# Weight preparation moved into the first round of layer 0, score and maximum banks lent in the first and last round of layer 1, its loop over two rounds, a re-ordered round

## The chip, the cores and the metric

One core of a Trainium2 chip runs the whole program. The metric is the device time of one execution in microseconds (us); the time before is the median of three runs.

## The reference

Sixteen sequences of 512 tokens with 128 features go through two layers, each of which adds an attention part and a feed-forward part to its input.

```python
xn = _layernorm(x)                       # layer 0
x = x + _L0_attn_ref(xn, ...) + _L0_ffn_ref(xn, ...)
xn = _layernorm(x)                       # layer 1
x = x + _L1_attn_ref(xn, ...) + _L1_ffn_ref(xn, ...)
```

`_L0_attn_ref` is a gated linear recurrence with 16 heads of 64 (products with Wq, Wk, Wv, Wg, a scan with a decay per head, Wo) followed by a GELU block. `_L0_ffn_ref` is a gated product with ternary weights, two hidden 512x512 products (h1, h2) and w3. `_L1_attn_ref` is gated linear attention with 4 heads in chunks; `_L1_ffn_ref` is softmax attention with 16 heads of 8 over 512 keys, a layer norm, and one of four expert blocks for each token.

## The kernel before, in words

The program has four parts, one after the other. **Setting up layer 0** (L655 to L737): a block loads the constants; `prepare_weights` (L41 to L98) brings the 3.9 MB of weights to be split in five chunks through two buffers, multiplies them with a bias vector on TensorE (L70, one column each, 36 products), scales them on ScalarE (L80), and splits them on VectorE into a rounded high part (L96) and a rest, the low part (L98); a third block adds the biases (L731 to L734). Each block ends with all engines together. **Layer 0** (`layer0_sequences`, L161) runs rounds -1 to 17: in a round the stages P, M, T and X work on different sequences, in the order that `layer0_order` writes out by hand. P is layer norm (`stats`, seven small POOL steps, `xn`), two transposes and four `gate` products; M the products with the scan (`v`, `k`, `g`, `q`), `wo` and `h1`. In round -1 only P lives. **Layer 1's attention** (`attention`, L890) works likewise in rounds -4 to 16. **The experts** (`experts`, L1787) work on the sorted tokens at the end.

A full round of `attention` has 32 positions p (`attention_order`, L771). Each begins with a `score` and a `max` step. `max` (stage B, for the next sequence): TensorE multiplies with 24 rows into the two MAX banks (L1307), VectorE takes the row maximum of both (L1597), and the next `max` product waits until it has. `score` (stage C): TensorE multiplies with 25 rows into the two SCORE banks (L1325), ScalarE takes the exponential (L1444), and the next `score` product waits for it. After them each position has other steps, put there by hand: `pv` (L1335, probabilities times values), `aoT` (L1343, a transpose, then L1603 and L1605 on VectorE), `h2` (L1196 to L1198, eight steps of two thirds of a dozen products, with a ScalarE copy after each odd one), `U` (L1247) and its states on VectorE (L1559 to L1564), `A` (L1257) with a mask on VectorE (L1569), `xT` (L1214), `mT` (L1313, the transpose of the maxima, with ScalarE's copy L1440), `oT` (L1282), `gwo` (L1289), and so on. Single banks for these are taken in turn from the ring 6, 7: there are 31 uses in a round, so that `gwo` (p=31) and `gz` (p=0 of the next round) both have bank 6, and `gz` waits until VectorE has read `gwo` (L1591).

In round -1 stage B lives and stage C does not, in round 15 stage C lives and stage B does not. In the rounds -1, 13, 14 and 15, `warm` steps stand at the even positions: five products (L1185) whose result nobody reads.

SyncE issues all loads and stores in the same order: after `mqklo` (p=19) the 24 stores `qk_st`, then the loads `Bld` for the next sequence, then `g1_ld` (two loads of 1 MB for the next `h2`). POOL issues the indirect stores `scatter` at p=31.

`run` (L1028) has the rounds -4 to 1 and 12 to 16 written out, and a loop whose body is one round for 2 to 11:

```python
for r in range(-4, 2):
    rounds(0, r, live(r))
with eng.Fori(2, BATCH - 4) as b:
    rounds(b, 0, order)
for r in range(BATCH - 4, BATCH + 1):
    rounds(0, r, live(r))
```

Of the kernel before, what the change touches and what calls it, by code (L numbers as in the profile page):

```python
# [40 lines left out]
def prepare_weights(nc, name, raw_dram, split_hi, split_lo, chunks, bias_products=None, psum_bias=None, by_dim=(), base=0):  # L41

    widest = max(n for _, n, _ in chunks)
    with ExitStack() as ctx:
        raw = [ctx.enter_context(nc.sbuf_tensor(f"{name}_raw{i}", [P, widest * P], F32)) for i in range(2)]
        loaded = [ctx.enter_context(nc.semaphore(f"{name}_loaded{i}")) for i in range(2)]
        multiplied = ctx.enter_context(nc.semaphore(f"{name}_multiplied"))  # L50
        scaled = ctx.enter_context(nc.semaphore(f"{name}_scaled"))
        hi_done = ctx.enter_context(nc.semaphore(f"{name}_hi_done"))
        lo_done = ctx.enter_context(nc.semaphore(f"{name}_lo_done"))
        block = ctx.enter_context(nc.Block())

        @block.sync
        def _(sp):
            for i, (first, n, _) in enumerate(chunks):
                if i >= 2:
                    sp.wait_ge(lo_done, i - 1)  # L60
                sp.dma_start(raw[i % 2][:, 0:n * P], raw_dram[:, first * P:(first + n) * P]).then_inc(loaded[i % 2], 16)

        @block.tensor
        def _(pe):
            for i, (first, n, _) in enumerate(chunks):
                pe.wait_ge(loaded[i % 2], 16 * (i // 2 + 1))
                for blk, col, vec in bias_products or []:
                    if first <= blk < first + n:
                        w = raw[i % 2][:, (blk - first) * P:(blk - first + 1) * P]
                        nc.tensor.matmul(psum_bias[:, col:col + 1], w, vec, start=True, stop=True)  # L70
                pe.drain().then_inc(multiplied, 1)

        @block.scalar
        def _(act):
            for i, (first, n, scale) in enumerate(chunks):
                w = raw[i % 2][:, 0:n * P]
                act.wait_ge(loaded[i % 2], 16 * (i // 2 + 1))
                act.wait_ge(multiplied, i + 1)
                if scale is not None:
                    nc.scalar.activation(w, w, ACT.Copy, scale=scale).then_inc(scaled, 1)  # L80
                else:
                    act.drain().then_inc(scaled, 1)

        @block.vector
        def _(dve):
            for i, (first, n, _) in enumerate(chunks):
                w = raw[i % 2][:, 0:n * P]
                at = slice((first - base) * P, (first - base + n) * P)
                if first in by_dim:
                    w = w.rearrange("p (g j d) -> p g d j", j=4, d=8)  # L90
                    hi, lo = (s[:, at].rearrange("p (g d j) -> p g d j", d=8, j=4) for s in (split_hi, split_lo))
                else:
                    hi, lo = split_hi[:, at], split_lo[:, at]
                dve.wait_ge(loaded[i % 2], 16 * (i // 2 + 1))
                dve.wait_ge(scaled, i + 1)
                nc.vector.tensor_copy(hi, w).then_inc(hi_done, 1)  # L96
                dve.wait_ge(hi_done, i + 1)
                nc.vector.tensor_tensor(lo, w, hi.bitcast(F32), ALU.subtract).then_inc(lo_done, 1)  # L98


# [11 lines left out]
PREP_ROUNDS, PREP_PER_ROUND = 3, 4  # L112

# [47 lines left out]
def layer0_sequences(nc, psum, w_hi, w_lo, w_plain, col, bias, half_bias, decay, rows, ident, s1_half, s12_half, minus_half, eps,  # L161
                     d_x, d_x1, d_g1, d_sorted, prep_chunks, table_parts):
    with ExitStack() as ctx:
# [11 lines left out]

        def blk(w, i):
            return w[:, i * P:(i + 1) * P]

        OUTS = 4
        xin = sb("xin", [P, TILES, P])  # L180
# [35 lines left out]
        ga = sb("ga", [P, HID, SEQ])  # L216
        pad = sb("pad", [P, 1, PAY])
        prep_raw = sb("prep_raw", [P, HID * P])
        prep = sb("prep", [P, 2, HID * P], F32R)
# [12 lines left out]
        sems("P_filled", "M_filled", "T_filled", "wo_done")  # L232
        sems("gate_t", "h0_hi", "v", "t", "g1", "hT_hi", "ga", "xT_hi", "yT_hi")
# [41 lines left out]
        def _(sp):  # L275
            def rounds(base, add, now):
# [7 lines left out]
                for stage, kind, i in now:  # L284
                    if stage == "W":
# [4 lines left out]
                        if kind == "prep_ld":  # L290
                            sp.wait_ge(S["prep_lo"], n)
# [9 lines left out]
                    elif kind == "x_ld":  # L301
                        sp.wait_ge(S["xn"], upto(stage, 1, 0))
# [23 lines left out]
        def _(pe):  # L326
            def rounds(base, add, now):
# [5 lines left out]
                def take(u):  # L333
# [3 lines left out]
                    for back in range(3):  # L337
# [5 lines left out]
                        if same:  # L343
                            s, per, k = FREE[same[-1]]
                            pe.wait_ge(S[s], upto(stage_of[same[-1]], per, k, back))
                            return

                def product(out, w_blocks, x_hi, x_lo):
                    last = 3 * len(w_blocks) - 1
                    n = 0  # L350
# [420 lines left out]
def attention_order():  # L771
# [77 lines left out]
    for p in WARM_AT:  # L849
        put(p, "idle", "warm")  # L850
# [1364 lines left out]
```

## Time and profile before

| what | us |
|---|---|
| median of three runs (2694.82 to 2701.45) | 2697.13 |
| the profiled execution | 2709.48 |
| its span | 2707.7 |
| set-up and round -1 of layer 0 | 0 to 74 |
| layer 0 | 74 to 937 |
| set-up of layer 1, its rounds -4 to -2 | 937 to 1053 |
| round -1 of layer 1 | 1053 to 1143.5 |
| rounds 0 to 14 | 1143.5 to 2451 |
| round 15 | 2451 to 2509 |
| round 16 and the experts | 2509 to 2707 |

The span runs from the first instruction to the last; 1.8 us of the profiled execution lie around it. Rows of a timeline give start, duration, engine, line, operation, and in brackets the idle time of the engine before it with what ended it. PEclk is TensorE's granted clock, 1.00 for 2.4 GHz and 0.50 for 1.2 GHz.

### The profile page before, as it was taken

To read this page: it belongs to the slowest core of one execution; us is meant where nothing else is said; L and a number is where in the kernel's file an instruction comes from. 1 tells how busy PE (TensorE), PEld (TensorE's weight loads), DVE (VectorE), ACT (ScalarE), POOL (GpSimd) and SP (SyncE) were. 2 spreads that over 40 slices of the span, in tenths; PEclk is the share of its full clock that TensorE was granted. 3 is DMA by queue.
4 is the path that set the end of the run, shared out by engine and by line. 5 is a ranking of instruction groups with operands and counts; after the bars stand their busy time and mean duration, and the time that the engine had idled before them with its cause. 6 is when DMAs were issued, how large, how long until landed. Compare 5 with 4: busy or idle time off the path is not lost. (4 is left out here: it accounts for less than half of the span.)

```text
span 2707.7 us, 45139 instructions
## 1 busy us (share of the span) xinstructions
PE 2422.3 (89%) x14582; PEld 1672.5 (62%) x14582; DVE 1933.5 (71%) x3706; ACT 1338.1 (49%) x1926; POOL 594.3 (22%) x630
## 2 busy tenths in 40 slices
PE   3899999999999946899999999999999999999596
PEld 2788888888888734654555545554555555554395
DVE  3889888888888713667777777777777777772375
ACT  1444444444444312265666656665666666555242
POOL 0021112111221100102222221213221221212287
PEclk9999999999999968999999999999999999999798
DMA  4334432233223133323343334333333233211463
GB/s 153 125 115 127 127 100 76 76 119 104 80 76 111 43 135 98 101 75 96 118 130 93 86 101 136 99 88 104 117 116 103 82 107 106 65 51 32 140 228 104
DMA packets 195550, 280.31 MB, mean 104 GB/s; under 512 B 21672, under 2 KB 151161, under 8 KB 186880
## 3 DMA queue, kind: packets, MB, share of 16 engines
q1 hardware_dynamic: 189952, 266.47, 32.8%
q0 software_dynamic: 5504, 12.63, 1.3%
q8 instruction: 53, 0.87, 0.1%
q14 instruction: 41, 0.34, 0.0%
HBM read 148.65 MB, written 131.91 MB: 104 GB/s over the span
## 5 line engine op out<-in xcount | busy, mean ns | idle before, releaser
L1597 DVE TENSOR_REDUCE c_row_max<-b_psum 128x2 f32<-128x1024 f32 x512 | 624.3, 1219 | 286.2 <-PE b_psum L1307 264.7
L1444 ACT ACTIVATE c_prob<-b_psum 128x1024 f32<-128x1024 f32 x512 | 524.1, 1024 | 388.0 <-PE b_psum L1325 384.4
L1307 PE MATMUL b_psum<-c_bk,c_bq 24*128 24x512 f32 x1024 | 261.8, 507 | 55.1 <-DVE c_row_max L1597 38.5
L1325 PE MATMUL b_psum<-c_cq,c_ck 25*128 25x512 f32 x1024 | 261.3, 505 | 36.4 <-ACT c_prob L1444 31.5
L1335 PE MATMUL b_psum<-c_prob,c_v_aug 128*32 128x512 f32 x2048 | 283.5, 627 | 0.3
L1325 PEld LDWEIGHTS b_psum<-c_cq,c_ck 25*128 25x128 f32 x1024 | 96.3, 185 | 218.1 <-ACT c_prob L1444 109.7
L353 PE MATMUL a_psum<-a_yT_hi,a_w_hi 128*128 128x512 f32 x512 | 206.8, 404 | 8.3 <-issue 5.9
L353 PE MATMUL a_psum<-a_yT_hi,a_w_lo 128*128 128x512 f32 x512 | 203.7, 398 | 0.0
L353 PE MATMUL a_psum<-a_yT_lo,a_w_hi 128*128 128x512 f32 x512 | 203.6, 398 | 0.0
L1307 PEld LDWEIGHTS b_psum<-c_bk,c_bq 24*128 24x128 f32 x1024 | 97.0, 186 | 108.1 <-DVE c_row_max L1597 82.1
L459 ACT ACTIVATE a_g<-a_psum,a_cols 128x512 f32<-128x512 f32 x64 | 44.1, 689 | 238.5 <-PE a_psum L353 238.5
L517 DVE TENSOR_TENSOR_SCAN a_st_sb<-a_decay,a_kv_sb 128x512 f32<-128x512 f32 x128 | 157.2, 1228 | 4.4
L615 POOL TENSOR_TENSOR a_rs<-a_mv,a_eps 128x4 f32<-128x4 f32 x16 | 3.2, 201 | 664.2 <-DVE a_mv L540 664.2
L376 PEld LDWEIGHTS a_psum<-a_w_plain,a_outs 128*128 128x128 f32 x1024 | 134.3, 192 | 11.8
L1196 PE MATMUL b_psum<-c_g_hi,b_f_hi 128*128 128x512 f32 x256 | 119.4, 467 | 17.7 <-DMA b_f_lo<-f_split_scratch 11.6
L376 PE MATMUL a_psum<-a_w_plain,a_outs 128*128 128x128 f32 x1024 | 135.0, 275 | 0.0
L1749 POOL TENSOR_TENSOR c_o_ms<-c_o_ms,b_minus_half 128x16 f32<-128x16 f32 x16 | 46.6, 2910 | 385.0 <-DVE c_o_ms L1581 385.0
L514 DVE SCALAR_TENSOR_TENSOR a_kv_sb<-a_psum,a_bias,a_v_sb 128x512 f32<-128x512 f32 x128 | 95.5, 746 | 44.0 <-PE a_psum L353 23.2
L353 PEld LDWEIGHTS a_psum<-a_yT_hi,a_w_hi 128*128 128x128 f32 x512 | 97.1, 190 | 29.8 <-issue 8.7
L447 ACT ACTIVATE a_v_sb<-a_psum,a_bias 128x512 f32<-128x512 f32 x128 | 88.7, 693 | 47.2 <-PE a_psum L353 46.2
L353 PEld LDWEIGHTS a_psum<-a_yT_lo,a_w_hi 128*128 128x128 f32 x512 | 97.6, 191 | 23.2
L353 PEld LDWEIGHTS a_psum<-a_yT_hi,a_w_lo 128*128 128x128 f32 x512 | 97.6, 191 | 21.2
(298 smaller groups left out, 5419.9 us busy)
## 6 DMA issues: line engine op xcount, KB each, us to landing
sorted_scratch<-a_pad SPq DMA_DIRECT2D x16, 2184.5 KB, 13.9
g_scratch<-a_g_hi SPq DMA_DIRECT2D x16, 1024.0 KB, 4.0
g_scratch<-a_g_lo SPq DMA_DIRECT2D x16, 1024.0 KB, 7.1
c_g_hi<-g_scratch SPq DMA_DIRECT2D x16, 1024.0 KB, 6.1
c_g_lo<-g_scratch SPq DMA_DIRECT2D x16, 1024.0 KB, 8.1
stack_scratch<-c_qk_hi SPq DMA_DIRECT2D x256, 64.0 KB, 1.6
d_wt<-expert_scratch SPq DMA_DIRECT2D x19, 834.0 KB
c_bq<-stack_scratch SPq DMA_DIRECT2D x128, 96.0 KB
```

The source lines that it names most:

```text
L353: mm = nc.tensor.matmul(out, a, c, start=(n == 0), stop=(n == last))
L376: mm = nc.tensor.matmul(tok[:, cut(t)], outs[:, i % OUTS, cut(t)], blk(w_plain, A_WO + i), start=(i == 0 and t == 0), stop=(i == FB0 - 1), ...
L447: nc.scalar.activation(v_sb[:, i % 2, :], bank(f"v{i}"), ACT.Identity, bias=bias[:, 4 * i:4 * i + 1]).then_inc(S["v"], 1)
L514: nc.vector.scalar_tensor_tensor(out=kv_sb[:, :], in0=bank(f"k{i}"), scalar=bias[:, 4 * i + 1:4 * i + 2], in1=v_sb[:, i % 2, :], op0=ALU.a ...
L517: nc.vector.tensor_tensor_scan(st_sb[:, :], decay[:, i:i + 1].to_broadcast([P, SEQ]), kv_sb[:, :], 0.0, ALU.mult, ALU.add).then_inc(S["sca ...
L1196: nc.tensor.matmul(bank(f"h2{c}"), hi, g1_hi[:, k, :], start=(k == 0), stop=False)
L1307: mm = nc.tensor.matmul(psum[:, MAX + x, :], bq[r, j, cut(t)], bk[r, j, :], start=True, stop=True)
L1325: mm = nc.tensor.matmul(psum[:, SCORE + x, :], ck[r, j, cut(kb)], cq[r, j, :], start=True, stop=True)
L1335: mm = nc.tensor.matmul(psum[32 * g:32 * g + 32, PV, :], v_aug[:, kb, HPG * j + g, :], prob[:, (2 * i + g // 2) % 4, g % 2, :], start=(kb ...
L1444: nc.scalar.activation(prob[:, i % 4, :, :], psum[:, SCORE:SCORE + 2, :], ACT.Exp, scale=DH1 ** -0.5).then_inc(S["exp"], 1)
L1597: nc.vector.tensor_reduce(row_max[:, t, at:at + 3:2], psum[:, MAX:MAX + 2, :], AX.X, ALU.max).then_inc(S["row_max"], 1)
L1749: nc.gpsimd.tensor_tensor(o_ms[:, 2, :], o_ms[:, 1, :], minus_half[:, :], ALU.pow).then_inc(S["o_rms"], 1)
```

## The change

Four things are done at once.

1. `prepare_weights` and the three set-up blocks of layer 0 go. SyncE issues the columns, the first input tile, the identity and all weight chunks at once, each with a semaphore and a place of its own. The high parts (ScalarE), the low parts (VectorE) and the bias products (TensorE) stand behind steps of round -1; round 0 begins with the bias sums.
2. In round -1 of layer 1 the odd `max` steps use the SCORE banks, in round 15 the odd `score` steps use the MAX banks; the product then waits for the reader of two steps before. `warm` stands at every fourth position in round -1, at the even ones in 13 and 14, and nowhere in round 15.
3. The loop's body holds two rounds; it runs five times in place of ten.
4. In every round of layer 1: the `h2` steps at even p stand first among the steps of their position and after `pv`, `ao` and `aoT` of stage C (before `aoT` of stage C2 at p=4, before `aT` at 6, before `xT` at 16), the one of p=14 moves to the end of p=13; `mT` 0 moves from 17 to 22, its store from 19 to 24; the second `oT` from 29 to 30. The banks up to `O1` are turned round: `gz` has bank 7, `gwo` bank 6, and the two neighbours in one bank are now `O1` and `mT` 0.

```diff
+WEIGHTS = {"s": (A_S1, 2 * HID, None), "q1": (0, 2 * FB0, "ln1_g"), "q2": (2 * FB0, 2 * FB0, "ln1_g"), "h1": (A_H1, HID * HID, None),
+           "w1": (A_W1, HID, "ln2_g")}
+HIGH_BEHIND = {("stats", 0): ("s", "q1", "q2"), ("gate", 0): ("h1",), ("gate", 1): ("w1",)}
+LOW_BEHIND = {("stats", 0): ("s",), ("xn", 0): ("q1",), ("gate", 0): ("q2",), ("gate", 1): ("h1",), ("gate", 2): ("w1",)}
+BIAS_BEHIND = {("stats", 0): range(0, 8), ("xT", 0): range(8, 12), ("gate", 0): range(12, 18), ("gate", 1): range(18, 24),
+               ("gate", 2): range(24, 30), ("gate", 3): range(30, 36)}
...
+            sp.dma_start(cols[:, :], d_cols).then_inc(S["cols_in"], 16)
+            sp.dma_start(xin[:, :, :], x_rows[0]).then_inc(S["x_in"], 16)
+            sp.dma_start(ident[:, :], d_ident).then_inc(S["ident_in"], 16)
+            for name in WEIGHTS:
+                sp.dma_start(raw_of[name], weight(d_split, name)).then_inc(S["raw_" + name], 16)
+            sp.dma_start(w_plain[:, :], d_plain[:, 0:A_W3 * P]).then_inc(S["plain_in"], 16)
+            sp.dma_start(rows[:, :, :], d_rows).then_inc(S["rows_in"], 16)
...
+                        nc.scalar.activation(weight(w_hi, name), raw_of[name], ACT.Copy,
+                                             scale=col(by) if by else 1.0).then_inc(S["w_hi"], 1)
...
+                        nc.vector.scalar_tensor_tensor(out=weight(w_lo, name), in0=raw_of[name], scalar=col(by) if by else 1.0,
+                                                       in1=weight(w_hi, name).bitcast(F32), op0=ALU.mult,
+                                                       op1=ALU.subtract).then_inc(S["w_lo"], 1)
...
-H2_AT = (2, 4, 6, 10, 14, 16, 19, 20)
+H2_AT = (2, 4, 6, 10, 13, 16, 19, 20)
...
+    for n, p in enumerate(H2_AT):
+        if p % 2 == 0:
+            put(p, "F", "h2", n)
     put(0, "C2", "xnb_ld")
...
-    put(17, "B", "mT", 0)
+    put(22, "B", "mT", 0)
...
-    put(19, "B", "m_st", 0)
+    put(24, "B", "m_st", 0)
...
-    put(29, "A1", "oT", 1)
+    put(30, "A1", "oT", 1)
...
+        bank_of |= {u: RING[(n + 1) % 2] for n, u in enumerate(ring_uses[:ring_uses.index("O1") + 1])}
...
-            few = r == -1 or BATCH - 3 <= r < BATCH
-            return [step for step in order if (few if step[0] == "idle" else 0 <= r + OUT_OF[step[0]] < BATCH)]
+            every = {-1: 4, BATCH - 3: 2, BATCH - 2: 2}.get(r)
+            return [step for step in order
+                    if (every and step[2] % every == 0 if step[0] == "idle" else 0 <= r + OUT_OF[step[0]] < BATCH)]
...
-            with eng.Fori(2, BATCH - 4) as b:
+            with eng.Fori(2, BATCH - 5, 2) as b:
                 rounds(b, 0, order)
+                rounds(b, 1, order)
...
-                        pe.wait_ge(S["row_max"], upto(stage, PAIRS, i))
+                        alone = not looped and add == -1
+                        pe.wait_ge(S["row_max"], upto(stage, PAIRS, i - 1 if alone else i))
...
-                        pe.wait_ge(S["exp"], upto(stage, PAIRS, i))
+                        alone = not looped and add == BATCH - 1
+                        pe.wait_ge(S["exp"], upto(stage, PAIRS, i - 1 if alone and i else i))
```

## Rows read from the trace of the kernel before

**Rows 1.** The page: the span of the profiled execution.
```profile
span 2707.7 us, 45139 instructions
```
**Rows 2.** Busy time by stretch: length, busy time of each engine, PEclk, DMA share, GB/s.
```profile
0.00:74.10 74.10, 25.83 (x104) 21.77 (x104) 27.68 (x52) 13.55 (x16) 3.23 (x11) 1.00 0.47 146
...
1053.30:1143.50 90.20, 78.13 (x393) 53.65 (x393) 55.72 (x72) 24.18 (x39) 10.10 (x8) 0.92 0.33 95
...
2451.40:2509.00 57.60, 54.79 (x300) 25.44 (x298) 9.88 (x45) 34.59 (x37) 10.97 (x13) 1.00 0.10 31
```
**Rows 3.** Timeline of the start, all engines.
```profile
13.20 14.04 PE L70 MATMUL a_psum<-a_cols,a_raw 128*128 128x1 f32 x64 [13.20 <-DMA a_raw<-in_a_split]
...
27.36 2.00 ACT L80 ACTIVATE a_raw<-a_raw,a_cols 128x2048 f32<-128x2048 f32 x1 [5.05 <-PEq L71]
...
43.22 2.29 DVE L98 TENSOR_TENSOR a_w_lo<-a_raw,a_w_hi 128x2048 fp32r<-128x2048 f32 x1
...
47.58 0.50 SPq L303 DMA_DIRECT2D a_xin<-in_x  x1
...
51.55 0.87 DVE L535 BATCH_NORM_STATS2 a_stats<-a_xin 128x6 f32<-128x128 f32 x4 [4.44 <-DMA a_xin<-in_x]
...
61.28 0.76 PE L353 MATMUL a_psum<-a_xT_hi,a_w_hi 128*128 128x512 f32 x1 [1.49 <-DVE a_xT_lo L502]
...
74.19 0.47 PE L353 MATMUL a_psum<-a_yT_hi,a_w_hi 128*128 128x512 f32 x1 [2.36 <-DVE a_yT_lo L502]
```
**Rows 4.** Groups of TensorE, then VectorE, 1053.4 to 1143.5 (round -1 of layer 1).
```profile
L1185 PE MATMUL b_psum<-b_f_hi 128*128 128x512 f32 x80 | 24.8, 446 | 0.0
L1307 PE MATMUL b_psum<-c_bk,c_bq 24*128 24x512 f32 x64 | 16.7, 517 | 18.5 <-DMA c_bk<-stack_scratch 10.0 <-DVE c_row_max L1597 8.3
...
L1597 DVE TENSOR_REDUCE c_row_max<-b_psum 128x2 f32<-128x1024 f32 x32 | 39.1, 1222 | 38.1 <-PE b_psum L1307 38.0
```
**Rows 5.** Round 15: ScalarE's largest group, and busy time of L1185 alone.
```profile
L1444 ACT ACTIVATE c_prob<-b_psum 128x1024 f32<-128x1024 f32 x31 | 31.7, 1024 | 23.6 <-PE b_psum L1325 22.8 <-PE b_psum L1335 0.6 <-issue 0.2
...
2451.40:2509.00 57.60, 22.58 (x80) 13.80 (x80) 1.00 0.10 31
```
**Rows 6.** Busy time by stretch: rounds 5, 7 and 12, and one piece of round 7.
```profile
1581.40:1667.00 85.60, 79.08 (x541) 44.31 (x541) 65.13 (x119) 53.83 (x74) 21.04 (x20) 0.98 0.36 108
...
1754.20:1842.80 88.60, 81.19 (x541) 45.87 (x541) 65.24 (x119) 53.94 (x75) 21.01 (x20) 0.96 0.35 104
...
2192.60:2279.80 87.20, 80.59 (x541) 45.73 (x541) 65.29 (x119) 53.88 (x74) 21.03 (x20) 0.96 0.30 83
...
1792.00:1798.80 6.80, 6.80 (x34) 3.90 (x34) 4.52 (x8) 1.02 (x1) 3.80 (x3) 0.50 0.00 1
```
**Rows 7.** Timeline of TensorE in round 7, from p=4, 14, 17, 22, 29 and 31.
```profile
1765.20 0.66 PE L1343 MATMUL b_psum<-b_ident,c_ao_sb 128*128 128x128 f32 x4
...
1790.49 0.50 PE L1307 MATMUL b_psum<-c_bk,c_bq 24*128 24x512 f32 x2 [0.54 <-DVE c_row_max L1597]
1791.90 1.98 PE L1257 MATMUL b_psum<-c_qg,c_kg 32*128 32x128 f32 x16 [0.91 <-DVE c_states L1564]
...
1804.53 0.60 PE L1313 MATMUL b_psum<-b_ident,c_row_max 128*8 128x128 f32 x4
...
1821.50 0.50 PE L1325 MATMUL b_psum<-c_cq,c_ck 25*128 25x512 f32 x2 [0.89 <-ACT c_prob L1444]
...
1835.84 1.09 PE L1282 MATMUL b_psum<-b_ident,c_o_n 128*128 128x128 f32 x8
...
1838.59 0.50 PE L1325 MATMUL b_psum<-c_cq,c_ck 25*128 25x512 f32 x2 [0.67 <-ACT c_prob L1444]
```
**Rows 8.** DMA queues: the loop from 1420 to 2190, then round 12.
```profile
q0 software_dynamic: 1536, 4.21, 1.4%
issues: line engine op xcount, KB each, median us to landing
...
q8 instruction: 4, 0.07, 0.3%
```

More of the change, by code:

```diff
@@ L38 @@
 OUT_SCALE0 = 0.5 * DH0 ** -0.5
[L41 to L98, printed above, removed]
@@ L174, in cut, with col, cols_of, weight @@
             return slice(t * P, (t + 1) * P)
+        def col(name, i=0):
+            return cols[:, A_AT[name] + i:A_AT[name] + i + 1]
+        def cols_of(name):
+            return cols[:, A_AT[name]:A_AT[name] + dict(zip(A_COLS, A_COLN))[name]]
+        def weight(w, name):
+            first, n, _ = WEIGHTS[name]
+            return w[:, first * P:(first + n) * P]
         def blk(w, i):
@@ L346, in take, with bias_products @@
                             return
+                def bias_products(kind, i):
+                    steps = [step[1:] for step in now]
+                    at = steps.index((kind, i))
+                    for n in BIAS_BEHIND.get(steps[at - 1], ()) if at else ():
+                        if n in (0, 16, 32):
+                            pe.wait_ge(S["raw_" + ("q1", "q2", "w1")[n // 16]], 16)
+                        block, by = (A_QKVG + n, "ln1_b") if n < 4 * FB0 else (A_W1 + n - 4 * FB0, "ln2_b")
+                        mm = nc.tensor.matmul(tok[:, n:n + 1], blk(raw, block), col(by), start=True, stop=True)
+                        if n == 4 * FB0 + HID - 1:
+                            mm.then_inc(S["bias_sum"], 1)
                 def product(out, w_blocks, x_hi, x_lo):
@@ L360, in turned @@
                     return mm
+                if not looped and add == 0:
+                    pe.wait_ge(S["w_lo"], len(WEIGHTS))
+                    pe.wait_ge(S["bias"], 3)
+                    pe.wait_ge(S["wo_scaled"], 1)
                 for stage, kind, i in now:
                     filled = S.get(stage + "_filled")
+                    if not looped and add == -1:
+                        bias_products(kind, i)
                     if kind in ("v", "k", "g", "q"):
@@ L397, in rounds @@
                     elif kind == "gate":
+                        if i == 0 and not looped and add == -1:
+                            pe.wait_ge(S["w_lo"], 1)
                         if i == 0:
@@ L431, in turn_on, with weights_high @@
                     act.wait_ge(S[stage + "_filled"], upto(stage, len(uses[stage]), uses[stage].index(u) + 1))
+                def weights_high(kind, i):
+                    for name in HIGH_BEHIND.get((kind, i), ()):
+                        act.wait_ge(S["raw_" + name], 16)
+                        by = WEIGHTS[name][2]
+                        nc.scalar.activation(weight(w_hi, name), raw_of[name], ACT.Copy,
+                                             scale=col(by) if by else 1.0).then_inc(S["w_hi"], 1)
+                if isinstance(base, int) and add == 0:
+                    act.wait_ge(S["bias"], 3)
                 def h0_high(stage, i):
@@ L849, in attention_order @@
     for p in WARM_AT:
-        put(p, "idle", "warm")
+        put(p, "idle", "warm", p)
     order = []
@@ L1320, in rounds @@
                             pe.wait_ge(S[f"m_in{i // STEPS}"], upto(stage, 32, 32))
-                        pe.wait_ge(S["exp"], upto(stage, PAIRS, i))
+                        alone = not looped and add == BATCH - 1
+                        pe.wait_ge(S["exp"], upto(stage, PAIRS, i - 1 if alone and i else i))
+                        if i == 0 and not looped and add == 0:
+                            pe.wait_ge(S["row_max"], PAIRS)
+                        if i == 1 and alone:
+                            pe.wait_ge(S["row_max"], PAIRS * BATCH)
                         j, kb, g2 = i // 8, i // 2 % TILES, i % 2
```

123 lines of the change are left out of this document (64 added, 59 removed).

## The prediction, made before the change was run

> **What bounds the kernel now.** I read the page first for the span [rows 1], then busy time by stretch, to give each of the four edits its own stretch [rows 2], and then inside each stretch whichever view shows what ends the waits there. The chain of waits is of no use here: it only follows the experts back, which the change doesn't touch. Its four edits meet four different bounds.
>
> The start is a chain of blocks: in 74.1 us TensorE is busy 25.8, VectorE 27.7, ScalarE 13.6 [rows 2]. The first weights land at 13.2, the last low part is made at 43 to 45.5, only then is the first input tile asked for (47.6), its statistics start at 51.6, the first gate product at 61.3, the first product of round 0 at 74.2 [rows 3]. Round -1 of layer 1 takes 90.2 us, with VectorE busy for 55.7 [rows 2]: the 32 maxima need 39.1 us and VectorE waits 38.0 for their products, while TensorE spends 24.8 us in products nobody reads [rows 4]. Round 15 takes 57.6 us with ScalarE at 34.6 [rows 2]; it waits 22.8 us for score products, and 22.6 us are again the unread products [rows 5]. The full rounds are TensorE's: busy 79 to 81 us of 85.6 to 88.6 [rows 6].
>
> **The start.** The first tile is now asked for at about 1.2 instead of 47.6, so its statistics could start at about 5.2 (the 4 us from issue to statistics of [rows 3]). Behind them the old path took 9.7 us to the first gate product. Now ScalarE first makes the high parts s, q1, q2 (1 + 2 + 2 us by L80's 2.00) before it may copy the transposed tile, and it waits for 2.5 MB to land, at some 12 us (the first MB landed 4.7 us after its issue). That puts the first gate product at about 17. The gate steps took 12.9 us (61.3 to 74.2) and are a chain of ScalarE and VectorE; two low parts of 2048 columns (2.29 each by L98) and one of 512 (0.7) are put between them on VectorE, 5.3 us, and the h1 high part and part of the bias products beside them, 1 more. The bias sums and the scaling of Wo come before round 0, 1.2. Sum 17 + 12.9 + 5.3 + 1 + 1.2 = 37.4; the pad store of 2 MB shares the DMA engines with the weights, so I take 38. **Saved: 36**, between 28 (chunks land 8 us later) and 41.
>
> **Round -1 of layer 1.** Of 16 groups of unread products 8 go; a group at full clock takes 1.25 to 1.4 us, two of them stood in half-clock stretches, in all 12. TensorE's waits for a maximum make 8.3 [rows 4] and mostly go, since the product now waits for the reader before last. After that TensorE has some 66 us of work and VectorE 55.7, coupled by one step of lead, and new waits of some 4 appear where VectorE has its long steps. **Saved: 16.5**, between 8 (the clock falls with less filling) and 22. What comes late next: the stores and loads for round 0 take SyncE some 20 us after p=19, and the shorter tail still has about 24; the order `Bld`, `g1_ld`, `m_st` leaves `m_st` behind both, also inside 24. I count nothing for it.
>
> **Round 15.** All 80 unread products go (21.6 us from start to start), 2.8 us of idle time too: TensorE has 33 us of work, ScalarE 34.6. With two bank pairs both run side by side; with one step of lead I take 38.5 us. **Saved: 19**, between 12 and 22.
>
> **The order, 15 rounds.** At p=14 TensorE waits 0.54 for the maximum and 0.91 for the states [rows 7]. The h2 step (1.5 us) moved to the end of p=13 fills these, but VectorE's own queue there (states, two masks, four normalizations, maxima) then sets the end at p=16, so half of it is gained: -0.7. `mT` (0.53 from start to start) moves from p=17, where TensorE has no idle time, to p=22, where it waits 0.89 for ScalarE [rows 7]: -0.5. The second `oT` (half of 1.03) goes to p=30, where the next score waits 0.67: -0.4. Against this, at p=4 `aoT` now stands behind h2: its 0.25 + 0.29 us on VectorE come later, the gate logarithms behind them too, and the maximum of p=5, for which p=6 already waits: +0.75. The turned ring lets `gz` start 0.5 us earlier, but the next maximum product waits for VectorE all the same: 0. Sum -0.85 a round. Then the clock: a stretch of 3.4 or 6.8 us at 1.2 GHz follows the idle time of p=14 in most rounds (1792 to 1798.8 in round 7 [rows 6]); a round with one takes 88.6, one with hardly any 85.6, so the average round loses about 1.7 there. I take a third of it as gone, -0.5. **Saved: 15 x 1.35 = 20**, between a loss of 8 (+0.5 a round: only p=4 shows) and 45 (all of the clock and the full 0.85).
>
> **The loop.** Round 12, written out, takes 87.2 at a clock of 0.96, round 7, in the loop, 88.6 at the same clock [rows 6]: a back edge costs at most 1.4. Five fewer save up to 7. On the other side, no instruction packet is fetched in the loop from 1420 to 2190, while a written-out round fetches four of 16 KB on one queue alone [rows 8]: the body of one round stays on the engines. Whether two do, no row shows. If not, the target of each of four taken back edges has to be fetched: by the nearest rows, a transfer takes from 1.6 us (the smallest stores) to 4 from issue to use, so 6 to 16 in all. **I take 0**, between -7 and +16.
>
> The Trainium skill, "Runtime: NRT & Kernel Launch", section Instruction fetch mechanics, says that TensorE's instruction memory holds 2048 instructions in blocks of 256, that it is filled ahead in order, and that a taken branch to a place outside it waits for a fetch. One round has 541 products and 541 weight loads [rows 6], so by that rule one round fits and two, 2164 and more, don't; that no packet is fetched in the old loop agrees. By the rule the term is +3 (10 for four fetches less 7) instead of 0, and it speaks against this part of the change.
>
> **Sum.** 36 + 16.5 + 19 + 20 + 0 = 91.5. Against the profiled execution's 2709.5 (span 2707.7 and 1.8 around it) that is 2618. The profiled execution lies 12.4 above the median of the runs, so I predict 2697.1 - 91.5 = 2605.6, say 2605.
>
> **The rivals.**
> - *The clock comes back.* If the denser p=13 to p=16 keeps TensorE at 2.4 GHz, each round gains 0.85 and some 2 more: 15 x 2.85 = 43 instead of 20, so 2582. For it: round 5 had no half-clock stretch at p=14 and took 85.6. Against it: the wait moves to p=16, it doesn't vanish, and `A` remains 16 small products.
> - *Only the ends gain.* The order's gain is eaten by p=4, and the doubled body is fetched anew at each back edge (10 us, as above): 36 + 16.5 + 19 - 10 = 61.5, so 2636. For it: the +0.75 at p=4 is as well founded as the gains.
> - *The ends do not overlap.* If lent banks only move the wait (the clock falls in round -1, `pv` paces round 15), the two give 10 in place of 35.5: 2631.
> - *Slower.* The doubled body has at least nine 16 KB packets of TensorE's instructions (twice the four and more of a round), 45 over five passes. In written-out rounds they come unseen, but if each stopped the engine, at 2.5 us each (between 1.6 and 4) they cost 112, and the time is 2717. It decides from 92 / 45 = 2.0 us a packet. Against it: the written-out round 12 with the same packets takes no longer than a looped one.
> - *The change doesn't do what it says:* the loads asked for at the start could still arrive in one stream behind which the first tile waits; it is second in the queue, so this is in the range.
>
> **Chances.** Forecast 0.50, clock comes back 0.19, only the ends 0.22, ends don't overlap 0.06, slower 0.03. The range 2570 to 2642 holds the forecast with most of its bounds, and the three rivals' middles. 0.3%, 8 us, is about what a measurement of this kernel tells from no change: faster 0.96, same 0.01, slower 0.03.
>
> **What would show it.** The first product of round 0 at 38 (under 45); the statistics at 5. Round -1 at 74 with VectorE waiting under 22 for L1307. Round 15 at 38 with ScalarE over 85% busy. In full rounds no 0.91 before L1257, a wait at p=16 instead, a later L1343 at p=4, and rounds of 84 to 87. Instruction packets between the old 1420 and 2190, and a gap of all engines every second round, would show the fetch. Wrong it would be if the weights delay the first tile, if round -1 stays over 80, or if the looped rounds get longer.

## The result, and the profile after

| | us |
|---|---|
| before, median | 2698.28 |
| after, median (2652.39 to 2659.24) | 2656.06 |
| ratio, 95% interval | 0.9843 (0.9825 to 0.9862) |
| the same two kernels in a later batch (e9 below), ratio | 0.9897 (0.9865 to 0.9929) |

The change makes the kernel faster, by 42 us where 92 were forecast; 2656 lies outside the range of 2570 to 2642. In the later batch the same pair differs by only 26 us (2701.6 and 2675.6), and the two intervals don't overlap: why isn't known. By stretches of the two profiles:

| stretch | before | after | forecast of the saving | saved |
|---|---|---|---|---|
| start to the first maximum product of layer 1 | 1053.4 | 1016.6 | 36 | 36.8 |
| round -1 of layer 1 | 90.2 | 81.5 | 16.5 | 8.7 |
| rounds 0 to 14 | 1307.9 | 1306.6 | 20 | 1.3 |
| round 15 | 58.0 | 50.9 | 19 | 7.1 |
| round 16 and experts | 198.2 | 197.7 | 0 | 0.5 |

They sum to 54, not 42, because the profiled execution of before was 12 us above its median; e2 suggests where those 12 lie. The start did what was forecast in this execution. Everything else fell short, most of all the rounds 0 to 14 (by 19), then round 15 (by 12) and round -1 (by 8). First the page and the stretches of the kernel after (length, PE, PEld, DVE, ACT, POOL, PEclk, DMA share, GB/s): round -1, rounds 0 to 14, round 15, and one piece of round 15.

```profile
span 2653.3 us, 44473 instructions
...
1016.60:1098.10 81.50, 72.59 (x353) 49.60 (x353) 55.39 (x72) 23.92 (x39) 10.12 (x8) 0.82 0.35 103
1098.10:2404.70 1306.60, 1199.80 (x8078) 680.11 (x8077) 965.02 (x1715) 799.28 (x1089) 300.18 (x282) 0.97 0.34 99
...
2404.70:2455.60 50.90, 43.63 (x225) 14.14 (x228) 9.74 (x45) 33.40 (x37) 10.91 (x12) 0.70 0.10 31
2421.96:2439.02 17.06, 15.38 (x65) 3.75 (x63) 2.77 (x12) 10.14 (x11) 2.91 (x3) 0.50 0.00 1
```

Read PEclk against [rows 2]: round 15 fell from 1.00 to 0.70, round -1 from 0.92 to 0.82. A mean of 0.70 over 50.9 us is 0.30 x 2 x 50.9 = 31 us at 1.2 GHz, and one piece of 17 us stands at 0.50 throughout. (The half-clock times below are summed from the trace's record of the granted clock, and may differ by 1 from such a sum.)

The groups of round 15 show whom that hits, against [rows 5]:

```profile
L1447 ACT ACTIVATE c_prob<-b_psum 128x1024 f32<-128x1024 f32 x31 | 31.2, 1024 | 19.4 <-PE b_psum L1327 19.4
L1337 PE MATMUL b_psum<-c_prob,c_v_aug 128*32 128x512 f32 x124 | 24.0, 854 | 6.3 <-ACT c_ao_sb L1455 6.3
L1327 PE MATMUL b_psum<-c_cq,c_ck 25*128 25x512 f32 x64 | 16.4, 633 | 1.0 <-ACT c_prob L1447 0.9
```

The score products no longer wait for the exponentials (0.9), so the lent banks do what they are for. But ScalarE still waits 19.4 us for them (22.8 before): TensorE is the late one, with `pv` at 854 ns each (about 605 where the clock is full, e6 and e8), and it waits 6.3 us for `c_ao_sb`.

**Two new waits in every round, one at every back edge.** TensorE in round 5, from p=4 to the maximum product of p=6; VectorE in the same stretch; TensorE from p=31 of round 5 to p=0 of round 6; VectorE in p=31:

```profile
1540.93 0.60 PE L1345 MATMUL b_psum<-b_ident,c_ao_sb 128*128 128x128 f32 x4
...
1544.49 0.49 PE L1327 MATMUL b_psum<-c_cq,c_ck 25*128 25x512 f32 x2
1546.07 0.50 PE L1304 MATMUL b_psum<-c_bk,c_bq 24*128 24x512 f32 x2 [1.09 <-DVE c_row_max L1601]
```
```profile
1541.86 0.29 DVE L1609 TENSOR_TENSOR c_attn<-b_psum,c_den 128x128 f32<-128x128 f32 x1
1542.07 0.68 DVE L1525 TENSOR_TENSOR c_logsig<-c_logsig,c_z_log 128x512 f32<-128x512 f32 x1
1542.79 1.37 DVE L1529 TENSOR_TENSOR_SCAN c_cum<-c_ones_row,c_logsig 128x128 f32<-128x128 f32 x4
1544.19 0.69 DVE L1533 TENSOR_TENSOR c_z_log<-c_cum 128x512 f32<-128x512 f32 x1
1544.80 1.22 DVE L1601 TENSOR_REDUCE c_row_max<-b_psum 128x2 f32<-128x1024 f32 x1
```
```profile
1609.70 1.07 PE L1337 MATMUL b_psum<-c_prob,c_v_aug 128*32 128x512 f32 x8
1611.45 2.02 PE L1285 MATMUL b_psum<-b_w_plain,c_o_f 128*128 128x128 f32 x16 [0.69 <-DVE b_place L1666]
1616.84 0.79 PE L1327 MATMUL b_psum<-c_cq,c_ck 25*128 25x512 f32 x2 [3.36 <-issue]
```
```profile
1609.81 1.22 DVE L1601 TENSOR_REDUCE c_row_max<-b_psum 128x2 f32<-128x1024 f32 x1 [0.59 <-PE b_psum L1304]
1610.95 0.16 DVE L1663 TENSOR_TENSOR c_spot<-b_psum,b_place 128x16 f32<-128x16 f32 x1
1611.15 0.16 DVE L1666 TENSOR_TENSOR b_place<-b_place,b_psum 128x4 f32<-128x4 f32 x1
```

At p=6 the product waits 1.09 where it waited 0.34: behind `aoT`, VectorE makes the whole chain of gate logarithms (2.8 us, 1542.07 to 1544.88) before the maximum of p=5. At p=31 `gwo` waits 0.69 for VectorE's reading of `rank` (L1666, done at 1611.31), which stands behind the maximum; before, it waited for nothing. And at the end of rounds 3, 5, 7 and 9, and of these alone, the next score product is 3.33 to 3.53 us late with nothing named that released it ("issue"). The queues of the kernel after from 1420 to 2190 show what is new there; [rows 8] have only q0 beside the data for the same stretch:

```profile
q0 software_dynamic: 1728, 4.74, 1.7%
q8 instruction: 47, 0.77, 0.5%
q14 instruction: 42, 0.34, 0.2%
```

### The profile page after: what moved, and what is told of

Read it like the earlier page. It is cut to its first block and busy times, and to the rows that moved or that the text cites. A ratio compares the mean times of both kernels' runs of the same rounds, so it can differ in the third digit from the quotient of the medians.

```text
span 2653.3 us, 44473 instructions
## 1 busy us (share of the span) xinstructions
PE 2391.7 (90%) x14462; PEld 1653.1 (62%) x14462; DVE 1926.4 (73%) x3701; ACT 1341.1 (51%) x1927; POOL 584.2 (22%) x630
## 5 line engine op out<-in xcount | busy, mean ns | idle before, releaser
L562 DVE SCALAR_TENSOR_TENSOR a_outs<-a_t_sb,a_u_sb 128x512 f32<-128x512 f32 x128 | 103.5, 809 | 16.9
L1717 POOL TENSOR_TENSOR c_rs<-c_mv,b_eps 128x4 f32<-128x4 f32 x32 | 6.5, 202 | 481.1 <-DVE c_mv L1493 481.1
```

The source lines that it names most:

```text
L562: nc.vector.scalar_tensor_tensor(out=outs[:, i % OUTS, :], in0=t_sb[:, i % 2, :], scalar=1.0, in1=u_sb[:, :], op0=ALU.add, op1=ALU.mult).t ...
```

## The experiments

Twelve runs (e9 is the changed kernel again), in three batches, each batch on one chip beside the kernel before. Ratios are to the kernel before of the same batch.

| run | what it is | ratio (95%) | half clock, us: r -1, r 0-14, r 15 | r -1 | r 0-14 | r 15 |
|---|---|---|---|---|---|---|
| before | | 1 | 15, 92, 0 | 90.2 | 1307.9 | 58.0 |
| after | | 0.984 | 30, 82, 30 | 81.5 | 1306.6 | 50.9 |
| e1 | loop over one round | 0.978 (0.975 to 0.981) | 24, 64, 41 | 78.8 | 1300.7 | 56.3 |
| e2 | parts 1 and 2 alone | 0.981 (0.976 to 0.986) | 19, 61, 47 | 74.0 | 1295.8 | 58.4 |
| e3 | before, part 3 alone | 1.003 (1.001 to 1.006) | 14, 72, 3 | 88.6 | 1306.2 | 59.4 |
| e4 | aoT first at p=4 | 0.981 (0.977 to 0.984) | 37, 84, 31 | 88.1 | 1302.4 | 51.2 |
| e5 | one position in four filled in r 15, two groups more in r -1 | 0.988 (0.985 to 0.992) | 35, 87, 10 | 86.0 | 1318.9 | 53.2 |
| e6 | every second filled in r -1 and r 15 | 0.988 (0.985 to 0.992) | 18, 79, 0 | 85.4 | 1307.9 | 53.9 |
| e7 | mended order, one round | 0.973 (0.970 to 0.975) | 18, 79, 47 | 78.6 | 1279.9 | 58.4 |
| e8 | e7 and e5's filling | 0.971 (0.968 to 0.973) | 28, 61, 0 | 86.3 | 1275.0 | 48.7 |
| e9 | after, again | 0.990 (0.987 to 0.993) | 27, 70, 41 | 81.1 | 1316.8 | 56.2 |
| e10 | e8, h2 back at 14 | 0.979 (0.974 to 0.983) | 14, 61, 7 | 78.7 | 1282.3 | 51.7 |
| e11 | e8, mT back at 17 | 0.974 (0.970 to 0.979) | 32, 72, 3 | 86.4 | 1279.3 | 50.2 |
| e12 | e8, r -1 as after | 0.971 (0.967 to 0.975) | 28, 82, 3 | 82.6 | 1280.6 | 50.2 |

The stretches are of one profiled execution each, and the half clock varies from one to the next, so stretches are read together with it.

### e1: the loop over one round again

```diff
-            with eng.Fori(2, BATCH - 5, 2) as b:
+            with eng.Fori(2, BATCH - 4) as b:
                 rounds(b, 0, order)
-                rounds(b, 1, order)
```

> The changed kernel, but its loop runs over one round again (ten passes). In the changed kernel's trace every second looped round (3, 5, 7, 9) ends with TensorE idle for 4.0 to 4.2 us ahead of the next score product (0.69 in the rounds between), all engines get instruction packets there, and 3.4 or 6.8 us at half clock follow. Theory 'refetch': the body of two rounds doesn't stay on the engines, each of the four taken back edges costs about 3.4 us of waiting and 1 of half clock: this kernel takes 2656 - 18 = 2638 us, no instruction packet is moved in the looped rounds, and no round has more than 0.8 us idle ahead of p=0. Rival 'parity': the gap belongs to something done every second round (two-fold buffers, a late load), and stays: 2650 to 2660, with gaps of about 4 us still there. A third: a back edge is dear in any case, so ten of them at 1.4 us take the gain back: about 2650.

**Measured:** 2648.6 (before on this chip 2706.9), ratio 0.978. No round has idle time of "issue" ahead of p=0, and from 1420 to 2190 the queues move next to no instructions (3 packets, from 2147 on, when the loop has been left):

```profile
q8 instruction: 3, 0.05, 0.0%
```

'Parity' and the third theory fall: nothing is late every second round, and ten back edges show no wait.

### e2: the ends alone

The order, the ring and the loop of the kernel before, with parts 1 and 2 of the change (diff: parts 3 and 4 undone).

> Only parts 1 and 2 of the change (weights prepared in round -1, lent banks, fewer unread products); the order of a round, the ring and the loop over one round are those of the kernel before. Theory 'the ends carry it all': by the two profiles the start gives 37 us to the first maximum product of layer 1, round -1 8.6 and round 15 7.2, together 53, and the new order with the doubled loop costs more than it brings: 2698 - 53 = 2645 us, 11 less than the whole change, and rounds 0 to 14 sum to about 1296 us. That would also say that the profiled execution of the kernel before was 12 us dearer in its rounds than usual. Rival 'order pays': the order gives what was forecast (20) and only the loop takes it away: 2660 to 2665, rounds 0 to 14 sum to 1308 as in the profile of before.

**Measured:** 2652.5, ratio 0.981; span 2642.7. Round -1, rounds 0 to 14, round 15:

```profile
1012.10:1086.10 74.00, 67.51 (x353) 46.67 (x353) 55.03 (x73) 24.12 (x39) 10.09 (x8) 0.87 0.41 120
1086.10:2381.90 1295.80, 1194.25 (x8077) 671.34 (x8077) 966.44 (x1715) 797.28 (x1089) 300.15 (x282) 0.98 0.34 99
2381.90:2440.30 58.40, 51.29 (x225) 16.46 (x225) 9.71 (x44) 33.50 (x37) 10.88 (x12) 0.59 0.10 30
```

Rounds 0 to 14 took 1295.8 with the very order and loop that took 1307.9 in the profile of before, at a clock of 0.98 instead of 0.96. That would account for the 12 us by which the profile of before stands above its median; but this run's own profile is 8 us below its median (2644.5), so it is a fit and not shown. 'The ends carry it all' holds in this much: of the 20 us forecast for the order no more than 4 show anywhere. The order costs 5 us in the profiles (e1's rounds against this run's) and gains 4 in the medians (2648.6 against 2652.5, the intervals overlap), and the loop costs on top. The ends themselves are worth reading: round -1 has the 74 us of the forecast, at a clock of 0.87 (0.92 before), while round 15 at 0.59 takes 58.4, no less than the 58.0 with all 80 unread products in it.

### e3: the kernel before with the doubled body

> The kernel before with part 3 alone: a loop body of two rounds, five passes. Theory 'refetch': four gaps of 3.4 to 4 us of all engines at the back edges, instruction packets through the loop, 1 us of half clock behind each: 2698 + 18 = 2716 us. Rival: the gap needs the new order (its last bank of the ring), then no gap at the end of every second round and five saved back edges: 2691 to 2698.

**Measured:** ratio 1.003 (1.001 to 1.006), 9 us slower. The profiled execution shows four gaps of 1.81 to 2.17 us, in all 7.9, again only after rounds 3, 5, 7 and 9, with no other edit in the kernel; one of them, and the queues from 1420 to 2190:

```profile
1664.24 0.50 PE L1326 MATMUL b_psum<-c_cq,c_ck 25*128 25x512 f32 x2 [2.17 <-issue]
```
```profile
q8 instruction: 48, 0.79, 0.4%
q14 instruction: 43, 0.35, 0.1%
```

'Refetch' holds, at half its price here: 2 us an edge instead of 3.4 to 4. By e1 and e3 together the gap belongs to the body of two rounds, not to the new order. Nor is it the new order that makes it longer: e5 and e6 have the changed kernel's loop body as it is, and only the written-out rounds -1 and 15 differ; their gaps are 1.97 to 2.53 us. What the length hangs on is open.

### e4: aoT ahead of h2 at p=4

```diff
-        if p % 2 == 0:
+        if p % 2 == 0 and p != 4:
             put(p, "F", "h2", n)
...
+    put(4, "F", "h2", 1)
     put(4, "A1", "gz2")
```

> The changed kernel, but at p=4 the transpose aoT stands ahead of the h2 step, as before. In the changed kernel VectorE reaches the maximum of p=5 later by the time that aoT was moved back, and the maximum product of p=6 waits 1.08 to 1.26 us for it (0.34 before), with half clock at p=6 in seven of ten looped rounds (5.1 to 5.8 us long in place of 4.0). Theory 'one step moved behind another': the wait at p=6 is 0.35 again, which gives 15 x 0.75 = 11 us, and the half-clock stretches at p=6 go, which gives up to 10 more: 2635 to 2645 us. Rival 'VectorE's queue of gate logarithms is the cause, aoT is not': the wait at p=6 stays near 1.1, 2652 to 2658. Other possibility: the wait goes but the stretch of half clock only moves to another idle place: 2645.

**Measured:** ratio 0.981, against 0.990 for the unchanged kernel in a later batch (e9). The wait at p=6 is back at its old size: over 15 rounds the mean idle time there is 0.30 (1.00), the position 3.19 us (4.45), 19 us in all. But against the first profile of the changed kernel position 3 is 0.75 longer, 1 and 2 together 0.5, and rounds 0 to 14 gain only 4 us, with 84 us at half clock (82). Against its second profile (e9) they gain 14; there position 3 takes 4.26 us without this edit (3.11 in the first profile, 3.86 in e4), so its length is not the edit's doing. The wait's cause is shown; whether its half clock went elsewhere isn't, the expected 2635 to 2645 us were missed (2655.0), and the changed kernel was not run in this batch.

### e5 and e6: filling against the clock

```diff
-            every = {-1: 4, BATCH - 3: 2, BATCH - 2: 2}.get(r)
+            every = {-1: 4, BATCH - 3: 2, BATCH - 2: 2, BATCH - 1: 4}.get(r)
...
-                    if (every and step[2] % every == 0 if step[0] == "idle" ...
+                    if (every and (step[2] % every == 0 or r == -1 and step[2] < 8) if step[0] == "idle" ...
```

That is e5; e6 has `{-1: 2, BATCH - 3: 2, BATCH - 2: 2, BATCH - 1: 2}`.

> The changed kernel with a few of the unread products back: in round -1 of layer 1 also at p=2 and p=6, in round 15 at every fourth position (8 groups, 40 products). They add work: 2 x 1.25 and 8 x 1.25 us at full clock. So far round 15 without them took 50.9, 56.3, 58.4 and 51.2 us with 30, 40, 47 and 31 us at half clock; TensorE has 33 us of work in it at full clock. Theory 'clock': what ate the gain of round 15 is the half clock, and 10 us of filling keep the clock up: round 15 in 43 to 46 us, with under 10 us of half clock, and round -1 in 74 to 78; the total is 2656 - 8 = 2648. Rival 'order of waits': the products of pv wait for the exponentials in this sequence whatever the clock is, then the filling adds to it or hides in the waits: 50 to 60 us, half clock or not. Third: the clock still falls with this little filling: 55 to 62 us with over 20 at half clock.

> The changed kernel with the unread products of the kernel before in rounds -1 and 15 (every second position, 80 products each, 20 us at full clock), the lent banks kept. This parts the lent banks from the filling. Theory 'clock': round 15 has no half clock, TensorE has 33 + 21.6 = 55 us of work and is the bound: 54 to 56 us (58.0 before, whose 2.8 us of idle time go), round -1 80 to 84. Rival 'the banks bring nothing by themselves': 57 to 59 and 88 to 91 us, as before. Total 2650 to 2665.

**Measured.** Round 15 in e5 takes 53.2 with 10 us of half clock, in e6 53.9 with none. First the stretch of e6's round 15 and two groups of its TensorE, which waits for nothing any more; then the stretch and `pv` in e8, with one position in four filled:

```profile
2406.10:2459.90 53.80, 53.80 (x305) 25.45 (x308) 9.88 (x45) 34.40 (x37) 11.14 (x13) 1.00 0.10 30
...
L1181 PE MATMUL b_psum<-b_f_hi 128*128 128x512 f32 x80 | 22.7, 413 | 0.0
L1337 PE MATMUL b_psum<-c_prob,c_v_aug 128*32 128x512 f32 x124 | 16.6, 605 | 0.0
```
```profile
2379.60:2428.20 48.60, 42.37 (x265) 18.77 (x265) 9.46 (x43) 33.66 (x37) 10.94 (x12) 1.00 0.12 36
...
L1338 PE MATMUL b_psum<-c_prob,c_v_aug 128*32 128x512 f32 x124 | 16.6, 604 | 6.2 <-ACT c_ao_sb L1456 4.5 <-ACT c_prob L1448 1.7
```

"A quarter" is one position in four (40 products), half of the old filling. With all the filling the lent banks alone give 4 us (58.0 to 53.9); with none, half the round or more runs at 1.2 GHz and takes 50.9 to 58.4 in six executions, 55.2 on average; with a quarter 0 to 10 us do and the round takes 48.7 to 53.2 in five, 50.8 on average. The cleanest pair is e7 and e8, whose round 15 differs by the filling alone: 58.4 us with 47 at half clock, 48.7 with none. So the clock is the cause, but not at the size that I expected, 43 to 46: e5's own 53.2 lies in the range of the rival 'order of waits' (50 to 60), and that rival has a part in it. The part that I had left out is the 6.2 us that `pv` waits, mostly for ScalarE's copy of `ao`: 33 + 10.7 of filling (the 40 products from start to start) come to 44, and 48.7 is found. The totals do not show the gain: 0.988 for both, where e5 was expected at 2648 us and measured 2676.7, e6 at 2650 to 2665 and measured 2671.8, and the changed kernel itself stands at 0.984 and 0.990. Rounds 0 to 14 of e5 took 1319 with 87 us of half clock, which these edits don't touch. Round -1 isn't helped by two groups more (86.0, where 74 to 78 was expected).

### e7 and e8: the order mended

```diff
-    put(30, "C2", "rank")
...
     put(30, "A1", "oT", 1)
+    put(30, "C2", "rank")
```

and the edits of e1 and e4; e8 has those of e5 too.

> The changed kernel with a loop over one round, aoT ahead of h2 at p=4, and rank behind the second oT at p=30. The last is new: in the changed kernel gwo (p=31) waits 0.69 us in each round from 1 on, none before, because the second oT was moved behind rank, which turned the ring so that gwo has the bank of rank, and VectorE reads that (L1663, L1666) only after the maximum of p=31. Theory: idle time ahead of p=0 (counted at p=31) is 0.00 instead of 0.65 with one round in the body, at p=6 it is 0.30; TensorE's idle time sums to about 5.5 us a round (6.9 in the loop over one round, 6.8 in the kernel before), so rounds 0 to 14 take 15 x 1.3 = 20 us less than those of the kernel before at the same clock: 1285 or so, the total 0.974 of the kernel before. Rival: TensorE's clock gives it back (the idle time that is filled in one place shows as half clock in another), then rounds sum to 1295 to 1302 and the ratio is 0.978 as with the loop alone.

> The mended order and loop together with the quarter of the unread products: the version that should beat both kernels. If both theories hold, gains add: round 15 at 45, round -1 at 74 to 78, rounds 0 to 14 at 1285 to 1290: ratio to the kernel before 0.970 to 0.973. If only the order holds 0.975; if neither, 0.979 as with the loop over one round alone.

**Measured:** 2632.2, ratio 0.973 (0.970 to 0.975), and 2627.5, ratio 0.971 (0.968 to 0.973): both beat the kernel before and the change on record (on one chip, e12 below, nearly the same kernel as e8, measures 2625.8 against 2675.6 for the change). Of e8's stretches rounds 0 to 14 came out better than expected (1275.0 for 1285 to 1290), round 15 (48.7 for 45) and round -1 (86.3 for 74 to 78) worse; its gain over e7 is within the intervals. The stretch of rounds 0 to 14 in e7, and its TensorE at the end of round 4 (p=31) and at p=6 of round 5:

```profile
1091.00:2370.90 1279.90, 1196.69 (x8078) 676.22 (x8077) 964.53 (x1715) 796.69 (x1089) 299.77 (x282) 0.97 0.35 100
```
```profile
1512.45 1.06 PE L1337 MATMUL b_psum<-c_prob,c_v_aug 128*32 128x512 f32 x8
1513.44 1.83 PE L1285 MATMUL b_psum<-b_w_plain,c_o_f 128*128 128x128 f32 x14
...
1533.09 0.50 PE L1304 MATMUL b_psum<-c_bk,c_bq 24*128 24x512 f32 x2 [0.36 <-DVE c_row_max L1601]
```

`gwo` follows `pv` at once. TensorE's idle time is 5.55 us a round (6.77 before, 6.93 in e1), and this is kept: 1280 and 1275 us against e2's 1296, with more half clock in e7 than in e2. The rival, that the clock gives it back, falls (1295 to 1302 and 0.978 by it).

### e9 to e12: which moves pay

e10 puts the one h2 step back at p=14 behind `A`, e11 mT back at 17 and its store at 19, e12 drops the two groups more of round -1.

> The changed kernel as it is, beside the others on one chip, and its second profile: how far one execution stands for the kernel. If the clock decides as the runs so far say, round 15 takes 50 to 59 us with 30 to 48 of it at half clock, round -1 74 to 88 in step with its half clock, p=31 has 1.5 us idle and p=6 1.0 on average over 15 rounds; ratio to the kernel before 0.982 to 0.985. If the first profile was an odd one, the gaps at p=31 or p=6 differ by over 0.3 us.

> The mended kernel (one round in the loop, aoT first at p=4, rank behind oT, a quarter of the unread products) with the one h2 step back at p=14, behind A, as in the kernel before. Theory: moving it to p=13 is the step that pays most: p=13 to 16 take 11.8 us in all kernels with the move and 12.8 to 13.8 without, so this one loses 15 x 1 to 2 us, 15 to 30, and stands at 0.977 to 0.981 of the kernel before, with 1.36 us idle at p=14. Rival: the half clock that goes at p=14 only comes back elsewhere, then it loses under 8 us: 0.971 to 0.973.

> The mended kernel with mT back at p=17 and its store at p=19. The prediction had the move of mT to p=22 at 0.5 us a round; in the traces p=17, 18 and 22 together take 6.71 us before and 6.79 after: it bought nothing, as what left p=17 came back as 0.15 us of waiting at p=17, 0.07 at 18 and a longer p=18. Theory 'nothing': ratio within 0.002 of the mended kernel's 0.9705. Rival 'it does pay and something else at p=18 costs': 7 us more, 0.973, with p=22 idle 0.76 again.

> The mended kernel with the quarter of unread products in round 15 alone, round -1 as in the changed kernel. Round -1 took 86.0 and 86.3 us with two more groups, and 74.0 to 88.1 without. Theory 'round -1 is not helped by them': here 74 to 82, with round 15 at 48 to 53, total 0.968 to 0.970. Rival 'the length of round -1 is the chance of its clock, the two groups cost 2.5 us': anything from 74 to 88, total as for the mended kernel within 0.002.

**Measured.** e9: 2675.6, ratio 0.990, above what I expected (0.982 to 0.985); its gaps at p=31 (1.62 us on average, 1.56 in the first profile) and p=6 (1.01, 1.00) repeat, the back edges cost 3.48 to 3.80.

e10: 2640.0, ratio 0.979 (0.974 to 0.983). The wait comes back at p=14,

```profile
1568.23 1.16 PE L1254 MATMUL b_psum<-c_qg,c_kg 32*128 32x128 f32 x16 [0.92 <-DVE c_states L1568]
```

but p=16 then waits 0.04 instead of 0.85, so positions 13 to 16 have 1.41 us idle against 1.27, and take 12.1 us against 11.8 in e8 and 12.0 in e12. Moving h2 ahead of the states moves the wait two positions on, with 0.1 to 0.3 us gained. The medians differ by 12 to 14 us, but the intervals overlap, and the rows account for 2 to 5: this stays open. What pays there is another part of the same edit: h2 first at p=16 (idle 0.04 in e10, 0.59 before).

e11: 2635.8, ratio 0.974 (0.970 to 0.979), the intervals overlap with e8's. Positions 17, 18 and 22 take 6.76 us, 6.82 in e8. 'Nothing' holds by the rows.

e12: 2625.8, ratio 0.971, the same as e8; round -1 took 82.6 us with 28 us of half clock. Its length goes with its clock as a tendency (74.0 at 19 us, 88.1 at 37, but 86.3 and 82.6 both at 28), and the rival holds. Why round -1 finds the clock high in one execution and not in the next isn't settled.

## Why the prediction was wrong, step by step

Mean distance between score products and idle time in them, in us a round, over the 15 rounds of each trace (in brackets the idle time):

| positions | before | e2 (old order) | e1 (new order) | after | e7 (mended) |
|---|---|---|---|---|---|
| 4 to 6 | 8.59 (0.34) | 8.62 (0.35) | 9.66 (1.07) | 9.87 (1.00) | 8.63 (0.35) |
| 13 to 16 | 13.77 (1.95) | 12.78 (1.96) | 11.84 (1.27) | 11.87 (1.27) | 11.88 (1.26) |
| 17, 18, 22 | 6.71 (0.90) | 6.70 (0.90) | 6.81 (0.66) | 6.79 (0.66) | 6.77 (0.67) |
| 29 to 31 | 8.19 (0.62) | 8.22 (0.63) | 8.48 (0.82) | 9.42 (1.73) | 7.72 (0.23) |

- **The start: right, with a clock in it that I had not seen.** Forecast 38 for the first product of round 0, found 33.55, and 36.8 us saved up to layer 1 for 36. Statistics started at 4.40, the first gate product at 15.89 (17 expected). But of the twelve executions with this start six have the first product of round 0 at 33.6 to 35.2 and six at 40.6 to 41.5 (first maximum product of layer 1: 1012.1 to 1021.6), so 38 is the middle of two cases and met neither. The rows show what parts them. The same gate product in the changed kernel and in e1:

```profile
20.35 0.39 PE L335 MATMUL a_psum<-a_xT_hi,a_w_lo 128*128 128x512 f32 x1
```
```profile
21.72 0.63 PE L335 MATMUL a_psum<-a_xT_hi,a_w_lo 128*128 128x512 f32 x1
```

 0.39 and 0.63 us are what such products take where the record has the clock at 1.00 and at 0.50 (e7, 1024.3 to 1026.0 and 1020.6 to 1022.8). In the six early executions the short ones begin at 20 to 26 us, in the six late ones at 44 to 49, though e1's TensorE is busy in all 18.0 us from 16 to 34. The record of the granted clock begins only at about that rise (at 64.9 in the kernel before), so the 1.00 of the first line of [rows 2], and the PEclk of any start, says nothing about the time ahead of it. Why the clock rises early in one execution and late in another is open.
- **Round -1: the wait right, the clock not; 8.7 for 16.5.** It stayed over 80, which was named as a sign of being wrong. TensorE waits 2.2 us for maxima (8.3 in [rows 4]), but VectorE still waits 30.5 for its products (38.0 there, under 22 expected):

```profile
L1304 PE MATMUL b_psum<-c_bk,c_bq 24*128 24x512 f32 x64 | 16.1, 566 | 14.7 <-DMA c_bk<-stack_scratch 12.5 <-DVE c_row_max L1601 2.2
```

 At a clock of 0.87, with the old order (e2), the round took 74.0, as forecast; at 0.82 it took 81.5. The clock was the bound of 8, and about that came. Beside it stands a wait that I had not counted, for the load of the first h2 step at p=2:

```profile
1020.51 0.79 PE L1192 MATMUL b_psum<-c_g_hi,b_f_hi 128*128 128x512 f32 x1 [3.19 <-DMA c_g_lo<-g_scratch]
```

 That is e7, whose round -1 took 78.6. In the ten other executions with the new order this wait is 0.95 to 5.29 us (1.47 after), with the old order 1.57 before, 0.58 in e3 and none in e2. So it seems longer where h2 stands first at p=2, but it was there before too, and what the order costs here isn't shown.

- **Round 15: 7.1 for 19, outside its own bounds of 12 and 22.** "TensorE has 33 us of work, ScalarE 34.6 ... I take 38.5." The 33 were counted at full clock, with the unread products as pure loss. In fact they paid for the clock: without them the clock fell to 0.59 to 0.70 and 33 became 44 to 51. I had written this down only for round -1 ("the clock falls with less filling") and as a rival of 6%; for round 15, where all of them go, its bound should have been the time at 1.2 GHz. ScalarE is busy 66% of the round (33.4 of 50.9) for the 85% expected.
- **p=4: right in kind, 0.75 forecast, 1.0 to 1.3 found,** since half clock follows the longer wait (e2 to e1, before to after). It should not have been set off against gains as one term among six.
- **p=14 and 16: the number right, by luck.** Idle time -0.68 for -0.7, with the shorter half clock -0.9 (e2 to e1). I had it from moving one h2 step to p=13, half of 1.45 us being gained. In e10, without that move, idle time is 1.41 a round already (1.95 before): 0.54 comes from h2 standing first at p=16, which I had not priced, and the move itself brings 0.14, as 0.81 of the 0.95 us that it takes from p=14 comes back at p=16.
- **mT: wrong, 0 for -0.5.** `mT` fills idle time at p=22 (0.76 to 0.30), but p=17 is only 0.22 us shorter, with 0.15 of new waiting, and p=18 is 0.26 longer, 0.07 of it waiting. The rest of p=18 is not explained.
- **oT: wrong, +0.3 for -0.4.** The step that failed is the one that looked only at the step moved. The second `oT` was put behind `rank`, which changed who holds the bank before `gwo`. With `rank` behind `oT` it is 8.22 to 7.72, -0.5: the forecast was that of another order.
- **The clock in the rounds: nothing for -0.5.** Half clock left p=14 (13 and 14 together are 1.7 us shorter, idle time not counted), and p=6 and p=16 are 0.6 us longer each for it; 82 us in place of 92, and 61 in e2 with the old order. The upper bound of 45 for the order, too, is more than its own terms give: 15 x (0.85 + 1.7) = 38.
- **The loop: +13.7 for 0,** the four gaps of 3.33 to 3.53; the upper bound of 16 held, and both signs named for the fetch came. This is the doubled body fetched anew (e1, e3). The five saved edges bring nothing to set against it, since ten edges show no wait in e1. An edge costs 1.8 to 3.8 us in these runs, and packets inside the body come unseen: 45 of them at the 2.5 us of the rival "slower" would have been 112. The Trainium skill, "Runtime: NRT & Kernel Launch", section Instruction fetch mechanics, says that a taken branch whose target is outside the current window of two pages waits for a fetch, and that TensorE's instruction memory has room for 2048 instructions. Taken by the 2048, a body of 2164 doesn't fit and one of 1082 does, and these traces agree (no packets and no gap with one round, both with two); taken by two pages of 256, one round would not fit either, and e1 speaks against that. The page of the Trainium skill gives no price. I had taken the middle and not the rule that spoke against the edit.

So the forecast's 92 became 37 + 9 + 7 + 1 = 54 by profile, and 42 by medians. Three steps failed: round 15's work was counted at full clock (12 us), the order's moves were priced one by one without the steps and banks behind them, and the loop's fetch was put at nothing (the last two together 19 us). No rival alone gives 2656. "Only the ends gain" (2636) with "the ends do not overlap" on top of it would, 36 + 10 - 10 = 36 saved, 2661, but that sum was made afterwards.

## What to carry to other kernels

Products that nobody reads can be what keeps TensorE at 2.4 GHz: before they are removed, count the stage at both clocks, and try a part of it (here 40 of 80 nearly held the clock and gave 48.7 to 53 us, where none gave 51 to 58). A step moved in a hand-written order also moves every later holder of a rotating buffer, so see who holds the bank before each neighbour, and what stands ahead in the queue of the engine that empties it. A loop body that stays on the engines shows no wait at its back edge; a doubled one that doesn't stay there cost 1.8 to 3.8 us each time round here and saved nothing.

## What the runs showed that I had not expected

- The back edge's wait differs between kernels: 1.81 to 2.17 us in e3, 3.33 to 3.80 in the changed kernel, twice, 1.97 to 2.53 in e5 and e6 with the same loop body.
- Round 15 at a clock of 0.59 takes 58.4 us with 225 matrix products (e2), and 58.0 at 1.00 with 300 (before).
- The same order and loop took 1307.9 and 1295.8 us for 15 rounds in two executions, with 92 and 61 us at 1.2 GHz. A single profile can't judge an edit worth 12 us here.
- Half of the executions with the new start run TensorE's part of it at 1.2 GHz and reach the first product of round 0 some 6 us later.
